# Layer 1 of a graph network on one core: where the one-hots of an edge visit come from

## The reference

```python
h = (x @ W).reshape(n, NHEAD, OUT_FEATS)        # 4 heads of 64
h_l = (a_l * h).sum(-1)
h_r = (a_r * h).sum(-1)
e = h_l[row] + h_r[col]
e = jnp.where(e > 0, e, ALPHA * e)
ex = jnp.exp(e - m[row])                        # m: the largest e of a row
att = ex / (denom[row] + 1e-16)                 # denom: segment sum of ex
msg = att[:, :, None] * h[col]
out = jax.ops.segment_sum(msg, row, num_segments=n)
```

## Time and profile before

| What | Value |
|---|---|
| Median of 3 runs | 4209.23 us (4208.39 to 4214.93) |
| Span of the profiled execution, first to last instruction | 4207.4 us |
| Mean granted TensorE clock, whole span | 0.776 |
| PE, busy | 2730.2 us (65%) |
| DVE, busy | 2571.9 us (61%) |
| POOL, busy | 2199.0 us (52%) |
| ACT, busy | 1421.0 us (34%) |
| DMA queue of POOL | 279.12 MB, 24.7% of 16 engines |
| DMA queue of SP | 97.19 MB, 7.5% |

### The profile page before, as it was taken

The page is one execution under the profiler, slowest core; times in us unless marked ns, Lnnn a source line. Parts: engine busy times, 40 slices in busy tenths (PEclk is TensorE's granted clock), DMA queues, the critical chain, the costliest instruction groups (busy, mean ns, idle before and its releaser), DMA issues. The chain is left out here.

```text
span 4207.4 us, 47856 instructions
## 1 busy us (share of the span) xinstructions
PE 2730.2 (65%) x12850; PEld 2053.4 (49%) x12850; DVE 2571.9 (61%) x5963; ACT 1421.0 (34%) x4306; POOL 2199.0 (52%) x2162
## 2 busy tenths in 40 slices
PE   5476777577777653815666666666666655699984
PEld 4243444355555543614544444444444435599972
DVE  5346998677777786435455565556555567544438
ACT  6663000077777731113221111111111113333334
POOL 0466777666666602573256665666665641255530
PEclk9778887788989865957777777777777775699985
DMA  5332333233333223622223333333333354222234
GB/s 145 87 87 82 89 88 87 86 87 93 89 93 95 86 67 87 159 62 66 69 78 86 91 87 85 87 89 89 89 87 86 87 79 159 76 72 70 71 92 145
DMA packets 204009, 379.38 MB, mean 90 GB/s; under 512 B 48926, under 2 KB 131873, under 8 KB 203619
## 3 DMA queue, kind: packets, MB, share of 16 engines
q0 software_dynamic: 102192, 279.12, 24.7%
q1 hardware_dynamic: 101556, 97.19, 7.5%
HBM read 314.12 MB, written 62.05 MB: 89 GB/s over the span
## 5 line engine op out<-in xcount | busy, mean ns | idle before, releaser
L534 POOL DMA_INDIRECT arena<-h_table,arena x1712 | 1729.3, 1010 | 1082.5 <-issue 479.2
L548 DVE TENSOR_TENSOR arena<-arena,ps 128x260 f32 (+1 forms) x1712 | 719.3, 420 | 848.1 <-remote 355.2
L2196 PE MATMUL ps<-arena 128*128 128x260 f32 x1760 | 674.2, 527 | 376.2 <-DVE arena L548 162.2
L1216 PE MATMUL ps<-arena 128*128 128x256 f32 x1664 | 556.6, 451 | 243.4 <-DVE arena L548 133.3
L2196 PEld LDWEIGHTS ps<-arena 128*128 128x128 f32 x1760 | 411.7, 258 | 534.5 <-issue 249.7
L1216 PEld LDWEIGHTS ps<-arena 128*128 128x128 f32 x1664 | 326.6, 221 | 400.1 <-issue 237.5
L717 ACT ACTIVATE arena<-arena 128x112 f16<-128x112 f16 x1568 | 446.7, 375 | 94.5 <-DVE arena L983 77.9
L2045 ACT ACTIVATE ps<-arena 128x32 f32<-128x32 f32 x110 | 22.1, 201 | 1036.9 <-DVE arena L2109 909.5
L884 DVE TENSOR_SCALAR arena<-arena 128x128 f32<-128x128 f32 x832 | 289.5, 349 | 0.4
L2120 DVE TENSOR_TENSOR arena<-arena,ps 128x1024 f32<-128x1024 f32 x220 | 267.1, 1214 | 2.1 <-ACT ps L2045 2.1
L2570 ACT ACTIVATE arena<-ps,arena 128x128 f32<-128x128 f32 x456 | 143.6, 366 | 307.1 <-PE ps L2618 274.6
(11 more groups left out here) (525 smaller groups left out, 4486.5 us busy)
## 6 DMA issues: line engine op xcount, KB each, us to landing
arena<-h_table,arena POOLq DMA_INDIRECT x1712
arena<-in_L_ffn_w SPq DMA_DIRECT2D x32, 512.0 KB, 7.7
xn_table<-arena SPq DMA_DIRECT2D x14, 896.0 KB, 4.0
slot_out<-arena SPq DMA_DIRECT2D x21, 512.0 KB
arena<-y_rows SPq DMA_DIRECT2D x12, 896.0 KB, 9.5
h_table<-arena SPq DMA_DIRECT2D x7, 924.0 KB
h_table<-arena SPq DMA_DIRECT2D x7, 896.0 KB, 4.2
arena<-in_x SPq DMA_DIRECT2D x48, 128.0 KB
```

The lines of the kernel that those rows point to most:

```text
L534: pool.indirect_dma_start(slot[:, 0:width], None, table, bass.IndirectOffsetOnAxis(ap=idx, axis=0)).then_inc(done, 16)
L548: dve.tensor_tensor(to, to, bank(b, width), ALU.add).then_inc(gnn_add, 1)
L1216: pe.matmul(bank(n % V0_BANKS, D), hot_w[:, g % 2, u, :], rows[:, n % RING, :], start=True, stop=True).then_inc(gnn_ps, 1)
L2196: pe.matmul(bank(4 + (g * U + u) % GNN1_BANKS, ACC_W), hot[:, b, u, :], rows[r][:, u, 0:ACC_W], start=True, stop=True).then_inc(gnn_ps, 1)
```

## The change

The lanes of all visits, bf16, are written to DRAM as one long row (`visit_lanes`) at the end of the block before. SP then reads 1024 of them (8 visits) per group into all 128 partitions, two groups ahead. DVE compares them with the partition's number, which is the transposed one-hot, in f32, without a transpose (`hot_lanes`). ACT makes the other one-hot as Relu(1 - Abs(lane - number)), in nine instructions (`apart`, `match`), into three buffers instead of two. `look_up` multiplies f32 with f32, 8 columns instead of 24, so there are no parts to cut or add, and the score reads PSUM. The steps of `attend` move up by one add, and the register load on PE goes behind the look-ups. The sums use four banks (`sum_bank`: 4, 5, 6 and 0, which held the transposes).

```diff
@@ -72,7 +72,6 @@
-PARTS = 3
@@ -118,6 +117,7 @@
+        visit_lanes = dram("visit_lanes", (NV * P,), BF16)
@@ -454,7 +454,7 @@
-        GNN0_BANKS, GNN1_BANKS = 8, 3
+        GNN0_BANKS, GNN1_BANKS = 8, 4
@@ -1731,6 +1731,10 @@
         def visit_bank(j):
...
+        lane_made = sem("lane_made")
+        lane_rows = v_w[:, 0:NV // 2].bitcast(BF16).rearrange("p (v e) -> p v e", v=VT)
+        lane_cols = vv["cols"].rearrange("p (v f e) -> p v f e", v=VT, f=2)[:, :, 1, :]
...
             @block.sync
             def _(sp):
@@ -1739,8 +1743,11 @@
+                sp.wait_ge(lane_made, 1)
+                sp.dma_start(visit_lanes.rearrange("(v p e) -> p v e", v=VT, p=P), lane_rows).then_inc(vis_out, 16)
...
+                sp.wait_ge(vis_out, 16 * 5)
...
             @block.gpsimd
             def _(pool):
@@ -1830,6 +1837,8 @@
                     if c + 2 < LOOPS:
...
+                act.wait_ge(vis_cols, 4 * VT)
+                act.copy(lane_rows, lane_cols).then_inc(lane_made, 1)
...
             @block.vector
             def _(dve):
@@ -1989,17 +1998,15 @@
-        hot_b = [take(U * P // 2).bitcast(BF16) for _ in range(2)]
-        hot_t = take(U * P // 2).bitcast(BF16)
-        ident_b = take(P // 2).bitcast(BF16)
+        lanes = [take(U * P // 2).bitcast(BF16) for _ in range(2)]
+        hot_t = [take(U * P) for _ in range(2)]
...
-        lc_parts = take(BUCKETS * PARTS * 2 * GH // 2).bitcast(BF16)
-        look = take(U * 2 * GH).rearrange("p (u w) -> p u w", u=U)
-        r_max, r_rows = take(GH), take(GH * P)
+        r_max = take(GH)
...
-        hot = take(2 * U * P).rearrange("p (b u n) -> p b u n", b=2, u=U)
+        hot = take(3 * U * P).rearrange("p (b u n) -> p b u n", b=3, u=U)
+        r_rows = arena[:, place["at"] - GH * P:place["at"]]
@@ -2008,16 +2015,26 @@
-        lcp = lc_parts.rearrange("p (t q w) -> p t q w", q=PARTS, w=2 * GH)
-        LW = PARTS * 2 * GH
+        LW = 2 * GH
...
-        (rm_done, rm_ps, lc_done, hots_done, hott_ps, hott_done, look_ps, score_done, ex_done, msg_done,
...
+        (rm_done, rm_ps, lc_done, hots_done, hott_done, look_ps, score_done, ex_done, msg_done, den_in) = (
...
+        lane_in = [sem(f"lane{b}_in") for b in range(2)]
+        A = Steps(nc.scalar, sem("act_step"))
...
+        def sum_bank(n):
+            return (4, 5, 6, 0)[n % GNN1_BANKS]
...
+            @block.sync
+            def _(sp):
+                for g in range(GROUPS1):
+                    if g >= 2:
+                        sp.wait_ge(hott_done, g - 1)
+                    sp.dma_start(lanes[g % 2], visit_lanes[g * U * P:(g + 1) * U * P].partition_broadcast(P)
+                                 ).then_inc(lane_in[g % 2], 16)
...
             @block.gpsimd
             def _(pool):
@@ -2032,13 +2049,17 @@
             @block.scalar
             def _(act):
-                def keep_hot(g):
-                    act.wait_ge(hott_ps, g + 1)
-                    act.copy(hot_t, bank(0, U * P // 2).bitcast(BF16)).then_inc(hott_done, 1)
...
-                def widen_hot(g, b):
-                    act.wait_ge(hots_done, g + 1)
-                    act.copy(hot[:, b, :, :].rearrange("p u n -> p (u n)"), hot_b[b]).then_inc(hot_done32, 1)
+                def apart(g, of):
+                    if g >= 3:
+                        act.wait_ge(gnn_ps, (g - 2) * U + (SUMS_BEFORE + R * U))
+                    for u in range(U):
+                        n = g * U + u
+                        last = act.activation(hot[:, g % 3, u, :], of, ACT.Abs, bias=v_loc[:, n:n + 1], scale=-1.0)
+                    A.add(last)
...
+                def match(g):
+                    h = hot[:, g % 3, :, :].rearrange("p u n -> p (u n)")
+                    act.activation(h, h, ACT.Relu, bias=ones[:, 0:1], scale=-1.0).then_inc(hots_done, 1)
...
                 def weigh(g, r):
@@ -2048,17 +2069,17 @@
                 for g in range(2):
-                    keep_hot(g)
-                    widen_hot(g, g)
+                    apart(g, iota)
+                    A.settle()
+                    match(g)
...
                 for g in range(GROUPS1):
...
-                        keep_hot(g + 2)
...
-                        act.wait_ge(gnn_ps, g * U + (SUMS_BEFORE + (R + 1) * U))
-                        widen_hot(g + 2, g % 2)
+                        apart(g + 2, lanes_ps)
+                        A.settle()
+                        match(g + 2)
...
             @block.vector
             def _(dve):
@@ -2075,54 +2096,45 @@
                 V.then(dve.tensor_scalar(bound, bound, -LIFT - OTHER, None, ALU.add))
-                for q in range(PARTS):
-                    V.then(dve.tensor_copy(lcp[:, :, q, :], lc3))
-                    if q + 1 < PARTS:
-                        V.then(dve.tensor_tensor(lc3, lc3, lcp[:, :, q, :], ALU.subtract))
-                V.then(dve.tensor_copy(ident_b, ident))
...
-                def one_hot(g, b, lanes):
-                    wide = [P, U, P]
-                    dve.tensor_tensor(hot_b[b].rearrange("p (u n) -> p u n", u=U), lanes.unsqueeze(1).to_broadcast(wide),
-                                      v_loc[:, ds(g * U, U)].unsqueeze(2).to_broadcast(wide), ALU.is_equal
-                                      ).then_inc(hots_done, 1)
...
-                def attend(g, stage):
+                def hot_lanes(g):
+                    dve.wait_ge(lane_in[g % 2], g // 2 * 16 + 16)
+                    if g >= 2:
+                        dve.wait_ge(look_ps, g - 1)
+                    dve.tensor_scalar(hot_t[g % 2], lanes[g % 2], lane, None, ALU.is_equal).then_inc(hott_done, 1)
...
+                def attend(g, u):
...
-                    if stage == 0:
+                    look = bank(2 + b, U * LW).rearrange("p (u w) -> p u w", u=U)
+                    if u == 1:
...
-                        V.add(dve.tensor_reduce(look, bank(2 + b, U * LW).rearrange(
-                            "p (u q w) -> p u w q", u=U, q=PARTS), AX_X, ALU.add))
-                    elif stage == 1:
-                        V.settle()
...
-                    elif stage == 2:
+                    elif u == 2:
...
-                    elif stage == 3:
+                    elif u == 3:
...
-                    elif stage == 4:
+                    elif u == 4:
...
-                            dve.wait_ge(hot_done32, g + 1)
-                            one_hot(g + 2, b, lanes_ps)
-                    else:
+                            hot_lanes(g + 2)
+                    elif u in MSG_AT:
...
-                        q = (stage - 5) * HALF_U
+                        q = MSG_AT.index(u) * HALF_U
...
-                STAGES = 7
+                MSG_AT = 5, 6
...
                 for g in range(2):
-                    one_hot(g, g, iota)
+                    hot_lanes(g)
@@ -2130,15 +2142,15 @@
-                for stage in range(STAGES):
-                    attend(0, stage)
+                for u in range(U):
+                    attend(0, u)
                 for g in range(GROUPS1):
...
                     for u in range(U):
-                        add_sums(dve, g * U + u, tiles[u], ACC_W, 4 + (g * U + u) % GNN1_BANKS, SUMS_BEFORE + R * U,
+                        add_sums(dve, g * U + u, tiles[u], ACC_W, sum_bank(g * U + u), SUMS_BEFORE + R * U,
...
-                        if u >= U - STAGES and g + 1 < GROUPS1:
-                            attend(g + 1, u - (U - STAGES))
+                        if g + 1 < GROUPS1:
+                            attend(g + 1, u)
...
             @block.tensor
@@ -2162,38 +2174,29 @@
-                def flip_hot(g, b):
-                    pe.wait_ge(hots_done, g + 1)
-                    for u in range(U):
-                        last = pe.transpose(bank(0, P // 2, u * P // 2).bitcast(BF16), hot_b[b][:, u * P:(u + 1) * P],
-                                            ident_b)
-                    last.then_inc(hott_ps, 1)
...
-                def look_up(g, b):
...
-                    tiles = load_tiles(pe, g * U)
+                def look_up(g, tiles):
...
                     for u in range(U):
-                        last = pe.matmul(bank(2 + b, LW, u * LW), hot_t[:, u * P:(u + 1) * P],
-                                         lc_parts[:, ds(tiles[u] * LW, LW)], start=True, stop=True)
+                        last = pe.matmul(bank(2 + g % 2, LW, u * LW), hot_t[g % 2][:, u * P:(u + 1) * P],
+                                         lc[:, ds(tiles[u] * LW, LW)], start=True, stop=True)
                     last.then_inc(look_ps, 1)
...
-                flip_hot(0, 0)
-                look_up(0, 0)
-                flip_hot(1, 1)
+                look_up(0, load_tiles(pe, 0))
+                tiles = load_tiles(pe, U)
                 for g in range(GROUPS1):
-                    r, b = g % R, g % 2
+                    r = g % R
...
-                        look_up(g + 1, 1 - b)
-                    pe.wait_ge(hot_done32, g + 1)
```

(26 more changed lines are left out.)

## The result

The changed kernel takes 4168.91 us (median of 4 runs, 4156.61 to 4177.54) against 4208.81 for the kernel before (4 runs): ratio 0.9908, 95% interval 0.9883 to 0.9933, 40 us faster. I had forecast 119.

A forecast was written before the change was run, and what follows sets the result against it. POOL's gathers and freezes (late PE results during gathers) were taken to bound the stage. Consumers alone summed to -188, but POOL's 1100 + 116 + 13 = 1229, 119 less, set the time: 4209 - 119 = 4090 us, range 3980 to 4230.

The forecast's parts named there:

- Second limit: POOL in the layer 1 stage: 1100 of gathers, 116 of freeze pauses and 13 held up make 1229 us, 119 less.
- my bank's term: Fourth sum bank: sums five to eight finish during a freeze, shortening POOL's pause; 40 times 1.6, -64 us.
- The other term: POOL's gathers in the layer 1 stage: 880 at 1.25 us each, 1100 us.
- Steps 1, 2, 3: DVE's one-hot and reduction replaced, -96 us; eight transposes per group gone from PE, -92; sixteen f32 look-up instructions, +55.
- Step 4: Fourth sum bank lets sums five to eight finish during a freeze: 40 times 1.6, -64 us.
- Steps 5 and 6: ACT's one-hot by Abs and Relu, and SP's lane transfers of 256 KB per group: both cost nothing.
- Step 7: POOL's gathers held up by DVE's new lane operation: 0.24 us per group, 26, half on the path, +13 us.
- "Absorbed": Rival: freezes lengthen by what the engines save, the ring fills at the same pace; 4209 within 20, chance 0.12.
- The floor: Rival: freezes go with PE's burst between sums, POOL's gathers alone set the stage; 3983 us, chance 0.18.
- cold PE: Rival: at low clock PE's look-ups cost 188 ns each and the register load is exposed; 4277 us, chance 0.16.
- my signs of being right: Lane operation near 0.70 us, "remote" over 150 behind look-ups, POOL waiting 120 to 180, clock near 0.7, gathers over 948 ns.

The follow-up runs named there:

- experiment 1: Changed kernel and kernel before, each with only the first 32 gathers kept and arithmetic bounded: 3723.19 us changed, 3745.04 before.
- experiment 6: Kernel before with a fourth sum bank alone, exponentials in free look-up bank columns, with freezes: 4179.11 us against 4183.35, ratio 0.9987.
- experiment 5: Without freezes, against the kernel before: changed kernel again, 3685.80 us, ratio 1.0054; kernel before with a fourth sum bank alone, 3666.25, ratio 1.0004.
- experiment 3: Changed kernel with the eight look-ups of a group made one matmul, with freezes: 4136.02 us, ratio 0.9811.
- experiments 4: Without freezes: changed kernel with three banks 3684.23 us, with spread look-ups 3683.87; kernel before with four banks, one-hot lanes from arena, 3688.82, unaltered 3657.73.

## Why the prediction was right or wrong

The sign was right, the size was not: 40 us instead of 119. By its steps:

- **Second limit, the step that failed.** I set the stage at POOL's 1100, 40 freezes times 2.9, and 13: 1229. The rows I had said otherwise. POOL waited 292.4 us for sums before (269.1 + 23.3 in the earlier trace rows); it paused 115 times in the stage (gaps over 0.8 us in the trace, the one at its start left out), not only at the 44 long waits, and at 12 of these it ran on without a pause. After the change these waits are 236.0, in 90 pauses, where I had 116 in 40. A pause is 2.5 us in the mean before and after: the change made pauses fewer, not shorter as my bank's term had it. I had counted the pauses in one example and multiplied it, where the row with their sum was shown. The other term was wrong the other way: 32 of the 880 gathers lie ahead of the first sum, so POOL's floor is 848 at 1.25, 1060 and not 1100. That the error came out at 80 us is luck: with 1060 my own sum gives 1189 and a gain of 159. Put together from the trace, the stage after is 1058 for gathers and issue, 20 for the held ones, 224 of waiting beyond issue, less 20 of it ahead of the first sum, and 27 behind the last gather: 1309.
- **Steps 1, 2, 3** (-96, -92, +55). The lane operation took 764 ns (0.70 forecast), and the sixteen look-ups 2.3 us per group (256.9 in 110; 2.56 forecast), so 1.2 more than before and not 1.4. The durations were nearly right. Their worth on the path was not: without gathers all three together, and what else the change does, gave 28 us (experiment 1), at a higher clock. And little of it is on the path with POOL at 10 us per group: what the consumers save is longer waiting (L548 606.5 against 563.5).
- **Step 4** (-64). The bank alone gave 4 us, within what the measurement tells from nothing (experiment 6). POOL does start sooner after a freeze, as I wrote, but it waits as much in all: 110 pauses of 2.5 us.
- **Steps 5 and 6** (nothing). ACT's 3.3 us per group (233.3 + 124.3 in 108 groups) made nobody late, the sums' matmuls named ACT for 7 us in the trace; leaving out the transfers moved nothing without freezes (3686.79 against 3685.80 in another session).
- **Step 7** (+13). I had 26 us of held gathers and put half on the path. Without freezes all of it is: POOL is busy 26 us longer, and the changed kernel is 20 to 24 us slower than the kernel before. With them POOL is busy 20.0 us longer, but taking this away gained nothing against the changed kernel (ratios 0.9917 and 0.9908), so none of it shows. Of the Trainium skill's warning "DVE blocks DMA" (SBUF — State Buffer), read as the whole operation, I had made 77; the gather that meets the operation grew by 0.28 us for its 0.75 in the row of experiment 5, and per group it is 0.24.
- **Rivals.** "Absorbed" was the nearest in mechanism: freezes lengthen by what the engines save. What it lacked is that POOL's waits fell by 56 us all the same. Which part of the change did that is not settled: not the bank alone, not the lane operation; what PE has ahead of its sums matters (experiment 3), and the change took the eight transposes from between the sums, but no run left them out alone. The floor was wrong, as freezes stayed; cold PE as well: the clock is 0.71, but with the load moved (and the lane operation with it) the ratio stayed what it was (0.9917). "Absorbed" named 4209 within 20, so by its number it missed too. Of my signs of being right all held but one, POOL's waits: 120 to 180 us forecast, 236 measured.

The Trainium skill (SBUF — State Buffer, SBUF: two separate sides) has the rule that PE never waits and DMA contends with no engine. With freezes PE's results are late, and without gathers they are not (experiment 1); whether a port of this memory makes them, no run shows. Without freezes the traces agree with it for PE: 850 gathers in flight and no wait over 3 us.

## What to carry to other kernels

Where one engine's chain of work fills a stage (here POOL's gathers), write the stage as that engine's busy time, its issue and its waits, all from its one row, and ask of every part of a change which of the three it moves; savings on other engines are worth nothing until they show there. Count all pauses of that engine and not those of one example. A wide DVE operation with all its operands in the arena cost POOL's gathers about 0.24 us each time, whether it took 0.75 us or 1.22 (experiments 4 and 5); read one operand from PSUM, or give it to ACT, but a step earlier than it is needed. And time a change in more than one session before believing a gain of 1%: this one is 1% faster in one and 0.5% slower in the other.

## What was not expected of the hardware

- The same kernel on the same chips takes 4183 to 4213 us or 3658 to 3666, for whole sessions at a time. In the slower case PE's results come late while POOL gathers: in the changed kernel 40 waits over 3 us, up to 11.2. What sets a chip into either was not found.
- These late results do not go with bytes (an eighth of them, same waits), and in the one run that varied it their length goes with what PE has queued ahead of a sum (with one look-up, two instructions, no wait is over 4.5 us; with eight, sixteen instructions, they reach 11.2).
- An engine freed in such a stage gives less than its work: DVE lost 82 us, and its waits grew by 43. Freed of the lane operation's 82 us too, it gave nothing more.
